# Attention pipeline with new engine orders and a joined mem+z matmul, shared network in ten units on kept turned rows

## What is computed

```python
h = patches @ W.T + b                     # 768 -> 256, class token in front
q, k, v = split(layernorm(h) @ Wq.T), ...  # 4 heads of 64
attn = softmax(where(causal, q @ k.T, min)) @ v
sq = elu(q) + 1
A_mem = (sq @ mem) / (sq @ z + 1e-6)
g = sigmoid(betas)
h = h + (g * A_mem + (1 - g) * attn) @ Wo.T + bo
x = layernorm(h)
shared = silu(x @ shared_w1.T) @ shared_w2.T
gates = softmax of the top 2 of 8 of x @ gate_w.T
h = h + shared + sum over the 2 experts e of gate_e * silu(x @ w1_e.T) @ w2_e.T
```

## Time and profile before

| | us |
|---|---|
| median of 3 runs | 393.52 |
| the profiled execution | 393.42 |
| its span, first to last instruction | 391.6 |
| PE busy | 338.3 (86%) |
| DVE busy | 248.3 (63%) |
| ACT busy | 166.7 (43%) |
| POOL busy | 162.1 (41%) |
| mean granted TensorE clock | 0.923 |

### The profile page before, as it was taken

The page is one execution under the profiler, slowest core; times in us unless marked ns, Lnnn a source line. Parts: engine busy times, 40 slices in busy tenths (PEclk is TensorE's granted clock), DMA queues, the critical chain, the costliest instruction groups (busy, mean ns, idle before and its releaser), DMA issues.

```text
span 391.6 us, 9897 instructions
## 1 busy us (share of the span) xinstructions
PE 338.3 (86%) x3430; PEld 279.4 (71%) x3430; DVE 248.3 (63%) x559; ACT 166.7 (43%) x371; POOL 162.1 (41%) x232
## 2 busy tenths in 40 slices
PE   4588989898897777399989999999999999999950
PEld 2367878788786565288878888777777778777730
DVE  0147787878686745559999678975655565556540
ACT  1035665665775533544344355743333332333210
POOL 0235565667652211102932502556444543553131
PEclk9799999999996855579999999999999999999995
DMA  7644332345222110452266656532233223333221
GB/s 248 167 153 133 128 92 67 100 142 178 78 70 74 33 69 23 133 211 67 66 133 141 175 132 176 114 60 42 42 55 55 39 47 55 49 41 50 30 27 13
DMA packets 18401, 36.32 MB, mean 93 GB/s; under 512 B 3349, under 2 KB 11000, under 8 KB 18360
## 3 DMA queue, kind: packets, MB, share of 16 engines
q1 hardware_dynamic: 11992, 27.71, 22.1%
q0 software_dynamic: 6368, 8.03, 14.2%
HBM read 28.52 MB, written 7.21 MB: 91 GB/s over the span
## 4 chain that ended last, share of the span: by engine, by line
PE 60%; DVE 15%; POOL 9%; issue 5%; ACT 5%; DMA 4%; SPq 1%; ACTq 0%; POOLq 0%; DVEq 0%
PE bank L651 17%; PE bank L664 12%; PE bank L666 6%; PE bank L576 5%; PE bank L453 3%; POOL weights L884 3%; PE bank L591 3%; PE bank L433 3%; PE bank L490 2%; DMA weights<-in_out_bias 2%; PE bank L562 2%; PE bank L471 2%; ACT weights L754 2%; DVE weights L1007 2%; DVE hid_lo L1232 1%
## 5 line engine op out<-in xcount | busy, mean ns | idle before, releaser
L651 PEld LDWEIGHTS bank<-x_t,weights 128*128 x1200 | 84.0, 98 | 25.9
L651 PE MATMUL bank<-x_t,weights 128*128 128x128 f16 x1200 | 99.6, 219 | 0.0
L823 ACT ACTIVATE act_out<-bank 128x512 f32<-128x512 f32 (+1 forms) x74 | 42.8, 580 | 118.7 <-PE bank L651 82.8
L664 PE MATMUL bank<-weights,hid_hi 128*128 x200 | 76.3, 381 | 0.1
L964 POOL DMA_INDIRECT out_rows<-y,add_id x26 | 42.8, 1645 | 73.5 <-DVE y L1242 65.1
L1230 DVE TENSOR_SCALAR hid_hi<-act_out 128x512 f16<-128x512 f32 (+1 forms) x74 | 31.8, 430 | 57.1 <-ACT act_out L823 54.7
L666 PE MATMUL bank<-weights,hid_lo 128*128 x200 | 54.5, 273 | 0.0
L1232 DVE SCALAR_TENSOR_TENSOR hid_lo<-act_out,hid_hi 128x512 f16<-128x512 f32 (+1 forms) x74 | 50.8, 686 | 2.5
L1069 DVE SCALAR_TENSOR_TENSOR weights<-stage,weights 128x1024 f16<-128x1024 f32 x36 | 43.7, 1227 | 2.4 <-ACT weights L754 2.4
L433 PE MATMUL bank<-weights 128*111 128x256 f32 x132 | 35.0, 421 | 5.8 <-DMA weights<-in_w_embed 5.8
L754 ACT ACTIVATE weights<-stage 128x1024 f16<-128x1024 f32 x36 | 37.3, 1052 | 0.0
(11 more groups left out here) (136 smaller groups left out, 547.5 us busy)
## 6 DMA issues: line engine op xcount, KB each, us to landing
stage<-in_w_ffn SPq DMA_DIRECT2D x36, 512.0 KB, 4.7
weights<-in_patches SPq DMA_DIRECT2D x11, 333.0 KB, 3.0
x_rows<-rows SPq DMA_DIRECT2D x11, 111.0 KB
out_rows<-weights SPq DMA_DIRECT2D x10, 111.0 KB
out_rows<-y POOLq DMA_DIRECT2D x10, 111.0 KB, 3.1
weights<-in_w_embed SPq DMA_DIRECT2D x1, 768.0 KB, 4.6
weights<-in_w_qk SPq DMA_DIRECT2D x1, 512.0 KB
slot_rows<-x_rows,gather_id POOLq DMA_INDIRECT x26
```

What stands on the lines that cost most here:

```text
L651: mm = nc.tensor.matmul(o, weights[:, bass.ds(base + 2 * k * CHUNK + 2 * (col - col % D) + w * D + col % D, P)], x_t[:, b, (2 * x + k) * P ...
L664: nc.tensor.matmul(bank[5 + b][0:m, :], hid_hi[:, b, c * P:c * P + m], weights[:, bass.ds(at, 2 * D)], start=(c == 0), stop=False)
L823: nc.scalar.activation(d_, s_, ACT.Silu, scale=1.0 / (X_SCALE * W_SCALE)).then_inc(hid_acted, 1)
```

## The change

**Order of the engines in the pipeline.** ACT runs `norm2` one step later (tile s-5), after `copy_xln_t` while embedding goes on and after `copy_qkv` in the drain; `norm1` stands ahead of `tanh_q`; `exp_gap` is a further step later and behind `split_hi`. PE runs `mix_values` right behind `project`, then `turn_rows`, then `project_out` (in the drain `project_out` ahead of `turn_rows`). DVE runs `finish_sq` one step later (tile s-2) and behind `max_score`, `row_lo` one step later (tile s-5) behind it, `min_q`, then `split_lo` (in the drain at the very end), then `combine`, and `residual` behind `combine`. POOL's and SP's orders stay.

**mem and z in one matmul.** `s_mem_z` holds both, 130 columns for each half; the results go to bank 0 behind the scores, and the four z matmuls (L480) and a wait of `turn_xln` on `dens_ready` go.

**Kept turned rows.** `x2_t` keeps all turned rows of the pipeline (1221 columns) in a buffer of its own, `rows` becomes a ring of 4 tiles, and the shared network reads `x2_t` directly, without `turn` and `copy_x_t`, in 10 units of 119 tokens (the last has 113). The loops of the shared network on PE and of the slots on ACT and DVE are written out.

```diff
+ROWS = 4
+UNITS = 10
+UNIT = -(-TOKENS // UNITS)
...
-        rows = sb("rows", [P, NT, 2 * D], F16)
+        rows = sb("rows", [P, ROWS, 2 * D], F16)
+        x2_t = sb("x2_t", [P, 4, NT * T], F16)
...
-        LATE_SHARED = [0] + [1] * 10
-        LATE_SLOT = [2, 2, 2, 2, 1, 1, 0]
+        LATE_SHARED = [0] + [1] * (UNITS - 1)
+        LATE_SLOT = [2, 2, 2, 2, 2, 1, 0]
...
-                if t >= 3:
-                    pe.wait_ge(dens_ready, t - 2)
...
-                    nc.tensor.matmul(bank[7][0:T, D + k * P:D + (k + 1) * P], sq[:, t % 3, k],
-                                     s_mem[:, k], start=True, stop=True)
-
-                pe.wait_ge(xln_t_ready, min(t + 3, NT))
-                for k in range(KC):
-                    mm = nc.tensor.matmul(bank[1][0:T, 2 * k:2 * k + 2], sq[:, t % 3, k],
-                                          s_z[:, k], start=True, stop=True)
+                    mm = nc.tensor.matmul(bank[0][0:T, 2 * T + k * (P + 2):2 * T + (k + 1) * (P + 2)],
+                                          sq[:, t % 3, k], s_mem_z[:, k], start=True, stop=True)
...
+                if 0 <= s - 3 < NT:
+                    mix_values(s - 3)
+                if s < NT and 0 <= s - 5:
+                    turn_rows(s - 5)
                 if 0 <= s - 4 < NT:
                     project_out(s - 4)
-                if 0 <= s - 5 < NT:
+                if s >= NT and s - 5 < NT:
                     turn_rows(s - 5)
-                if 0 <= s - 3 < NT:
-                    mix_values(s - 3)
...
+            def shared_up(n):
+
+                m = tokens_of(n)
                 for half_ in range(2):
...
+                    if n >= 2:
+                        pe.wait_ge(hid_acted, 2 * (n - 2) + half_ + 1)
+                    up_half(n, half_, m, 0, lambda q: x2_t[:, q, n * UNIT:n * UNIT + m])
...
-            pe.wait_ge(h2_ready, NT)
-            turn(0, 0, rows[:, 0], T)
             pe.wait_ge(attn_ready, NT)
             pe.wait_ge(x2_t_ready, NT)
             wait_split(pe, CHUNKS)
-            up(0, 0, T, 0)
+            shared_up(0)
             ranks()
...
+            for n in range(1, UNITS):
+                shared_up(n)
+                if n < UNITS - 1:
+                    down(n - 1, (n - 1) % 2, tokens_of(n - 1), 0)
+                if n == 5:
+                    inverse()
...
+                if t >= ROWS:
+                    act.wait_ge(x2_turned, t - ROWS + 1)
+                    act.wait_ge(rows_out[t % ROWS], 16 * (t // ROWS))
...
-                for c in chunks_at(s - 1):
-                    split_lo(c)
+                if 0 <= s - 2 < NT:
+                    finish_sq(s - 2)
+                if 0 <= s - 5 < NT:
+                    row_lo(s - 5)
                 if 0 <= s - 1 < NT:
                     min_q(s - 1)
+                if s < NT:
+                    for c in chunks_at(s - 1):
+                        split_lo(c)
+                if 0 <= s - 3 < NT:
+                    combine(s - 3)
                 if 0 <= s - 4 < NT:
                     residual(s - 4)
-                if 0 <= s - 3 < NT:
-                    combine(s - 3)
                 if 0 <= s - 5 < NT:
                     top2(s - 5)
-                if 0 <= s - 1 < NT:
-                    finish_sq(s - 1)
-                if 0 <= s - 4 < NT:
-                    row_lo(s - 4)
+                if s >= NT:
+                    for c in chunks_at(s - 1):
+                        split_lo(c)
```

More of the change, by code:

```diff
@@ L130, in build @@
         share = part(2 * HEADS)
-        read = sb("read", [P, D])[:]
+        read = part(D)
         attn = part(2, D)
@@ L184, in build @@
         stage_in = [sem(f"stage_in{i}") for i in range(STAGES)]
-        rows_out = sem("rows_out")
+        rows_out = [sem(f"rows_out{i}") for i in range(ROWS)]
         h2_stored = [sem(f"h2_stored{i}") for i in range(4)]
@@ L601, in _ @@
             wait_split(pe, CHUNKS)
-            up(0, 0, T, 0)
+            shared_up(0)
             ranks()
-            turn(1, 1, rows[:, 1], T)
-            up(1, 1, T, 0)
-            turn(2, 0, rows[:, 2], T)
-            down(0, 0, T, 0)
-            def shared_pair(n):
-                for b in range(2):
-                    up(n + b, b, T, 0)
-                    turn(n + b + 1, 1 - b, rows[:, bass.ds(n + b + 1, 1)].rearrange("p a b -> p (a b)"), T)
-                    down(n + b - 1, 1 - b, T, 0)
-            with pe.Fori(1, 3) as i:
-                shared_pair(2 * i)
-            inverse()
-            with pe.Fori(3, (NT - 1) // 2) as i:
-                shared_pair(2 * i)
-            up(NT - 1, 0, T, 0)
+            for n in range(1, UNITS):
[4 more added lines that the diff above has]
+                    inverse()
             base_of = {}
@@ L629, in know, with rows_of @@
                                                       "expert_of is written")[1][0]
[L631 to L636 removed]
+            def rows_of(j):
+                pe.wait_ge(slot_rows_in[j % 4], 16 * (j // 4 + 1))
+                if j == 0:
+                    pe.wait_ge(h2_ready, NT)
+                turn(slot_rows[:, j % 4])
+            rows_of(0)
+            down(UNITS - 2, (UNITS - 2) % 2, tokens_of(UNITS - 2), 0)
             pe.wait_ge(experts_known, 1)
@@ L790, in _ @@
                     copy_xln_t(s - 1)
+                if s < NT and 0 <= s - 5:
+                    norm2(s - 5)
                 if 0 <= s - 4 < NT:
@@ L796, in _ @@
                     copy_qkv(s - 1)
+                if s >= NT and s - 5 < NT:
+                    norm2(s - 5)
+                if s < NT:
+                    norm1(s)
+                if 0 <= s - 1 < NT:
                     tanh_q(s - 1)
@@ L930, in _ @@
                 pool.wait_ge(h2_stored[q], 16 * len(range(q, NT, 4)))
-            for t in range(NT):
+            for t in range(UNITS):
                 if t == 2:
@@ L1252, in late_lo @@
                     split_lo(c)
-            split_hidden(0, 0, T, first=True)
+            split_hidden(0, 0, UNIT, first=True)
             dve.wait_ge(dummy_out, 16)
             find_slots()
-            for t in range(1, NT):
-                split_hidden(t, t % 2, T, first=(t == 1))
-                shared_y(t - 1)
-                if t == 2:
+            for n in range(1, UNITS):
+                split_hidden(n, n % 2, tokens_of(n), first=(n == 1))
+                shared_y(n - 1)
+                if n == 2:
@@ L1292, in _, with slot_y @@
-            SLOT_LOOP = (SLOT_TILES - 3) // 4
-            with dve.Fori(1, SLOT_LOOP) as i:
-                for r in range(3, 7):
-                    slot_step(4 * i + r, r % 4)
-            for j in range(4 * SLOT_LOOP + 3, SLOT_TILES):
-                slot_step(j, j % 4)
+                late_lo(n)
+            def slot_y(j):
+                output(UNITS + j, j % 2, P, y[:, j % 2], slot_gate[:, j:j + 1])
+            for j in range(SLOT_TILES):
+                split_hidden(UNITS + j, j % 2, P)
+                if j == 0:
+                    shared_y(UNITS - 1)
+                else:
+                    if j == 1:
+                        late_lo(UNITS + j)
+                        for q in range(3):
+                            dve.wait_ge(shared_out[q], 16 * len(range(q, UNITS, 3)))
+                    if j >= 3:
+                        dve.wait_ge(added, 16 * (j - 2))
+                    slot_y(j - 1)
+                if j != 1:
+                    late_lo(UNITS + j)
```

241 lines of the change are left out of this document (104 added, 137 removed).

## The result

| | us |
|---|---|
| before, median of 4 runs beside it | 393.37 |
| the changed kernel, median of 4 runs | 379.74 (379.61 to 379.88) |
| ratio | 0.966, 95% interval 0.964 to 0.968 |
| its profiled execution | 379.71, span 377.9 |

In the changed kernel's profile the lines have moved a little: on PE `embed` is L432, `mix_values` L470 and L474, `turn_rows` L442, `project_out` L484, `logits` L499, the units' ups and downs L570, L598 and L600, the slots' first matmul L647. On DVE `finish_sq` is L993 and L997, `row_lo` L1044, `min_q` L987, `split_lo` L1061, `residual` L1037, `embed_h` from L980. On ACT `norm1` is L755, `tanh_q` L738 and L742, `copy_x2_t` L721 (the profile calls what it writes x_t), `norm2` L769. On POOL `inv_std` is L868 to L874 and `relu_q` L882.

The account below looks back on a forecast made before the run. Pipeline bound by an engine-to-engine loop, then DVE with residual; units 0 to 5 by DVE, units 6 on and slots by PE. +0.4 - 9.5 + 0.8 - 5.9 + 0.3 = -13.9 from 393.42: 379.5, range 373.5 to 386.0.

Parts of the forecast that it names:

- Full pipeline, +0.4: Start of step 10's embedding, E(10), at 107.5 for 107.13, with step 5's, E(5), staying at 52.1.
- The step of 10.85: Full pipeline: time between embeddings, 10.2 plus 0.65 lost by DVE to POOL; a step with two splits 12.0.
- the term of 0.65: Full pipeline: DVE's loss per step to POOL's relu_q beside split_lo or L1030, taken as 0.65, bounds 0 and 1.0.
- The floor of 10.2: Full pipeline step without loss to POOL: 2.8 until embed_h, 7.3 of DVE work through residual's first instruction, 0.06 signal.
- the signs I named: Pipeline: embeddings 10.6 to 11.2 apart, released by residual; no xln-copy wait; split_lo or L1030's successor stretched beside relu_q.
- rivals 1 and 2: Full pipeline: POOL takes nothing from DVE (375.6, 22%); DVE waits for all of relu_q each step (381.5, 10%).
- Drain, -9.5: From E(10), step 10's embedding start, to the first up matmul: 49.0 instead of 58.5.
- my milestones: Drain, counted from E(10): steps 10 to 15 done at 12.1, 22.1, 30.1, 38.2, 43.2 and 49.0.
- Units 0 to 5, +0.8: Shared network, bound by DVE: split_lo behind top2(10) delays the members, costing 0.8, bounds 0 and 2.
- Units 6 on, -5.9: Shared network, PE-bound: one unit fewer -5.2, turns -0.8, wider columns +0.7, written-out loops -0.6.
- Rival 3: The clock drops at step 11, low through the drain (+3) and over up(1) and down(0) (+2): 384.5, 13%.
- Rivals 4 and 5: PE at 1.2 GHz in units 0 to 5 (403, 3%); new order doesn't bite, drain keeps 58.5 (389, 4%).

Follow-up runs that it names:

- run 1: The changed kernel with ACT's copy of the turned rows (copy_x2_t) ahead of norm1 and tanh_q instead of behind them: 374.86 us, ratio to before 0.953.
- run 10: The changed kernel with copy_x2_t first and late weight splits at other places, plus residual's addition ahead of combine's last two additions on DVE: 368.67 us, ratio 0.939.
- run 6: The changed kernel with eleven shared-network units of 108 tokens instead of ten of 119: 384.17 us, ratio to before 0.976.
- run 7: The changed kernel with the twenty late weight splits at other places, none in units 1 to 3: 376.92 us, ratio to before 0.960.
- Run 9: The changed kernel with each drain step's first split_lo ahead of row_lo, waiting for inv_std2, instead of behind top2: 377.76 us, ratio to before 0.959.
- Run 5: The changed kernel with the old order of pipeline work on PE, ACT and DVE; merged mem+z, kept rows and ten units stay: 384.44 us, ratio 0.977.

## Why the prediction was right, and where its steps were not

The total, 379.5, is 0.2 off, and the four large terms came out within half a microsecond each. That is better than the reasoning deserved.

- **Full pipeline, +0.4 (measured +0.9).** The step of 10.85 was met (10.83), the reason was not. The step that failed is the term of 0.65 that DVE was to lose to POOL in each step: DVE lost nothing, POOL lost 1.8, and the wait went by way of norm1, tanh_q and the copy to PE's logits. The floor of 10.2 under it was right (10.26 in run 1) and is residual's (run 10). The 0.65 and the real 0.57 (10.83 less 10.26) agree by chance. The rows for the right reading were at hand: in the earlier trace rows POOL's L884 lost 1.15 beside split_lo, and I read the group for what DVE could lose. I asked what stands beside relu_q, which moved, and not what stands beside inv_std1. Of that I had only noted that its second instruction no longer falls beside split_lo; its last one now falls beside the whole run. Of the signs I named, the intervals and the missing xln wait came; the embeddings released by residual and the stretched DVE instruction did not. Two differences cancel: E(5) came 1.05 earlier than forecast, and the five steps took 57.0 for 55.4, by the double split (12.44 for 12.0) and by the step behind it (12.03 for 10.85). Both excesses are the low clock: in run 6, where it fell only behind the double step, that step is 11.97, as forecast. The 1.05 is within what executions differ by: in the kernels whose first steps are those of the changed one E(5) lies between 50.51 (run 1) and 52.45 (run 7). The prediction's E(10) for rivals 1 and 2 (103.6 and 109.6) count six steps where there are five; by its own terms they are 104.3 and 109.3.
- **Drain, -9.5 (measured -9.5).** The first up at 49.05 behind E(10), forecast 49.0. Within it the steps ran ahead of my milestones (residual's statistics of step 14 done at 42.2 for 43.2) and the last one fell back: 6.9 for 5.8, as the split behind top2 held inv_std by 1.16 there. Run 9 shows this place worth 2.6; it is in no term of the prediction, which costed POOL at its length alone, 2.4. So the rest of the chain was costed about as much too high, and the drain's fit is partly luck. Run 5 splits the 9.5 in 6.7 of the order and 2.8 of the rest.
- **Units 0 to 5, +0.8 (+0.6)**, with PE waiting for hid_lo in units 3 and 4, as named; run 7 shows the bound is DVE. The members were later by the two splits, and PE waited 0.56 for them.
- **Units 6 on, -5.9 (-5.9)**; run 6 measures the unit and the columns together at 3.9. The parts for the turns and for the written-out loops were not tested by themselves.
- **Slots, +0.3 (+0.1).**
- **Rivals.** 1 and 2 were about DVE losing to POOL, none or all: the table had no case in which POOL loses, though its time would have been the same as mine. Rival 3 took part: the granted clock dipped at the end of step 8 and in step 9 but was 0.78 over the drain, above the 0.67 of that stretch before. Rivals 4 and 5 did not come.

## What to carry to other kernels

When two engines share something, ask of every short operation on the slower one what long run of the other now stands beside it, also where neither was touched, and follow who waits for it; a 0.27 operation set the step here. Ask it of DVE work that follows without a pause above all. A step has several loops of nearly equal length: take the longest out and read the trace again, since the next may be 0.6 behind. Where a forecast fits, check the reason by moving the thing blamed: here that, with the waits it uncovered, found 14.7 more.
